# A decoder layer with a mixture of experts on one core: first products of the experts two ahead, double buffers, weights loaded in two parts

## What is computed

```
h = layernorm(x)                                   # 1024 x 256
scores = sigmoid(h @ gate_weight.T)                # 1024 x 16
weight_matrix = top 4 of 16 scores in the best 2 of 4 groups, normalised, x 2.5, else 0
g = einsum('th,nfh->ntf', h, gate_w);  u = einsum('th,nfh->ntf', h, up_w)   # 16 routed experts, f = 128
routed = einsum('ntf,nhf,tn->th', silu(g) * u, down_w, weight_matrix)
shared = silu(h @ sh_gate_w.T) * (h @ sh_up_w.T) @ sh_down_w.T              # f = 256: two more experts of 128
x = x + routed + shared
```

## Time and profile before

| what | value |
|---|---|
| median of 3 runs | 598.18 us (596.38 to 601.23) |
| the profiled execution | 597.41 us |
| its span on the core | 595.5 us |
| PE busy | 557.4 us (94%) |
| DVE busy | 437.1 us (73%) |
| ACT busy | 398.3 us (67%) |
| POOL busy | 298.9 us (50%) |
| share of PE in the chain that ended last | 83% |

### The profile page before, as it was taken

The page is one execution under the profiler, slowest core; times in us unless marked ns, Lnnn a source line. Parts: engine busy times, 40 slices in busy tenths (PEclk is TensorE's granted clock), DMA queues, the critical chain, the costliest instruction groups (busy, mean ns, idle before and its releaser), DMA issues.

```text
span 595.5 us, 10331 instructions
## 1 busy us (share of the span) xinstructions
PE 557.4 (94%) x3392; PEld 488.2 (82%) x3392; DVE 437.1 (73%) x1046; ACT 398.3 (67%) x783; POOL 298.9 (50%) x201
## 2 busy tenths in 40 slices
PE   3899999999999999999999999897777799999996
PEld 1687889989989989989989988786566688888885
DVE  8778989989989988998998998968593433333334
ACT  4978988878978979879779778665531433343331
POOL 2434756746746646656666563301041655556542
PEclk9998999999999999999999999999998899999999
DMA  6122032032032032032031020110002433333311
GB/s 206 29 107 81 0 117 81 1 116 81 2 117 81 2 116 81 2 116 75 8 116 56 27 97 23 59 29 1 0 1 70 149 105 107 104 123 113 108 62 70
DMA packets 16267, 42.23 MB, mean 71 GB/s; under 512 B 4544, under 2 KB 4800, under 8 KB 16224
## 3 DMA queue, kind: packets, MB, share of 16 engines
q1 hardware_dynamic: 16224, 41.69, 20.9%
HBM read 40.47 MB, written 1.21 MB: 70 GB/s over the span
## 4 chain that ended last, share of the span: by engine, by line
PE 83%; DVE 8%; ACT 4%; DMA 2%; issue 2%; SPq 1%; ACTq 0%; DVEq 0%
PE bank L1258 20%; PE bank L1260 19%; PE bank L1259 19%; PE bank L1254 15%; PE bank L1396 5%; PE bank L1384 4%; ACT tok L624 2%; DMA xbias<-in_xb 1%; DMA w_raw<-in_w 1%; DVE stats L976 1%; DVE xT_lo L911 1%; DVE gated_lo L1158 1%; ACT values L538 0%; DVE x L1248 0%; DVE raw L995 0%
## 5 line engine op out<-in xcount | busy, mean ns | idle before, releaser
L1258 PE MATMUL bank<-xT_lo,w_hi 128*128 128x512 f32 x336 | 140.0, 417 | 3.6 <-DVE conv L1149 1.3
L1260 PE MATMUL bank<-xT_hi,w_hi 128*128 128x512 f32 x336 | 132.3, 394 | 0.0
L1259 PE MATMUL bank<-xT_hi,w_lo 128*128 128x512 f32 x336 | 131.8, 392 | 0.0
L425 POOL TENSOR_TENSOR gated_lo<-gated,gated_hi 128x512 fp32r<-128x512 f32 x30 | 38.7, 1290 | 116.5 <-ACT gated_hi L644 112.8
L624 ACT ACTIVATE tok<-bank,nmr,rstd 128x128 f32<-128x128 f32 x256 | 91.0, 504 | 2.1 <-DVE nmr L891 2.1
L502 POOL TENSOR_TENSOR gate<-conv,tap 128x512 f32<-128x512 f32 x36 | 46.4, 1291 | 84.5 <-DVE conv L1149 71.4
L1258 PEld LDWEIGHTS bank<-xT_lo,w_hi 128*128 128x128 f32 x336 | 63.5, 189 | 18.8 <-DVE conv L995 3.2
L1260 PEld LDWEIGHTS bank<-xT_hi,w_hi 128*128 128x128 f32 x336 | 63.3, 188 | 14.2
L420 POOL TENSOR_TENSOR conv<-tap,conv 128x506 f32<-128x506 f32 x32 | 61.9, 1934 | 21.8 <-DVE conv L995 21.8
L420 POOL TENSOR_TENSOR raw<-tap,raw 128x506 f32<-128x506 f32 x32 | 61.9, 1934 | 20.3 <-DVE raw L995 16.3
L1259 PEld LDWEIGHTS bank<-xT_hi,w_lo 128*128 128x128 f32 x336 | 63.7, 190 | 9.6
(11 more groups left out here) (167 smaller groups left out, 1358.3 us busy)
## 6 DMA issues: line engine op xcount, KB each, us to landing
w_raw<-in_w SPq DMA_DIRECT2D x34, 384.0 KB, 4.4
obet<-obet_rows SPq DMA_DIRECT2D x16, 768.0 KB, 4.2
tap<-route_rows SPq DMA_DIRECT2D x16, 512.0 KB, 3.6
wv_raw<-in_wv SPq DMA_DIRECT2D x8, 256.0 KB, 4.8
wo_raw<-in_wo SPq DMA_DIRECT2D x8, 256.0 KB, 4.9
x<-in_x SPq DMA_DIRECT2D x2, 512.0 KB, 4.6
out_x<-x SPq DMA_DIRECT2D x4, 256.0 KB, 2.4
raw<-in_ctx SPq DMA_DIRECT2D x1, 512.0 KB, 5.4
```

The lines of the kernel that those rows point to most:

```text
L425: nc.gpsimd.tensor_tensor(gated_lo[:, cc], gated[:, c * N:(c + 1) * N], gated_hi[:, cc].bitcast(F32), ALU.subtract).then_inc(gated_lo_read ...
L1258: nc.tensor.matmul(o, l_hi, r_lo, start=start, stop=False, skip_group_check=loose)
L1259: nc.tensor.matmul(o, l_lo, r_hi, start=False, stop=False, skip_group_check=loose)
L1260: return nc.tensor.matmul(o, l_hi, r_hi, start=False, stop=stop, skip_group_check=loose)
```

## The change

It has five parts, all in the expert block.

1. PE makes the first products two experts ahead: the loop is `gate_up(n + 2)`, `down(n)` in place of `gate_up(n + 1)`, `down(n)`. Around the router, `gate_up(1)` is cut into its four banks, `gate_up(3)` stands in one piece before the weights' transposes, and `down(2)` is split around them.
2. `silu_g`, `prod`, `act_w`, `act_hi`, `act_lo` have two buffers, used in turn. `act_high(n)` and `down_high(n)` wait for `down(n - 2)`.
3. A weight load is two transfers: gate and up (256 KB, `load_gate_up`) once the low part of expert n - 2's gate and up is made, and down (128 KB, `load_down`) once `down_low(n - 2)` is.
4. The shared experts are not multiplied with ones: POOL's memset and four `weigh` are gone, and `act_high` reads `prod`.
5. Experts 3 and 4 are split early: ACT makes their high parts (128 x 768 each) behind `context_soft(1)`, POOL their low parts once the first half of `x_mixed` is there, into the free tiles `wv_hi/lo` and `wo_hi/lo`. The loads of experts 5 and 6 follow at once, their low parts on POOL wait for the end of the router (`r_ready`).

```diff
             sp.wait_ge(w_lo_ready, H + 2)
             load_expert(4, 1)
+            for n in (5, 6):
+                sp.wait_ge(w_lo_ready, n - 2 + H)
+                load_expert(n, 1 - n % 2)
...
+            def load_route(e, s):
+                if not (isinstance(e, int) and e < 2):
+                    sp.wait_ge(e_weighted, e * NCH - NCH)
...
+            def load_gate_up(n, s):
+                sp.wait_ge(w_lo_ready, n + (H - 2))
...
+            def load_down(n, s):
+                sp.wait_ge(down_lo_ready, n - 6)
...
+            load_route(0, 0)
+            load_route(1, 1)
+            load_gate_up(7, 0)
+            load_route(2, 0)
+            load_down(7, 0)
+            load_gate_up(8, 1)
+            load_route(3, 1)
+            load_down(8, 1)
+            with sp.Fori(0, E_ROUTED // 2 - 3) as r:
+                for s in range(2):
+                    load_gate_up(r * 2 + (9 + s), s)
+                    load_route(r * 2 + (4 + s), s)
+                    load_down(r * 2 + (9 + s), s)
             for s in range(2):
-                load_route(s, s, NCH * (s + 1))
-            with sp.Fori(0, E_ROUTED // 2 - 1) as r:
-                for s in range(2):
-                    expert_split(r * 2 + (3 + s))
-                    load_expert(r * 2 + (5 + s), s)
-                    load_route(r * 2 + (2 + s), s, r * (2 * NCH) + NCH * (3 + s))
+                load_route(E_ROUTED - 2 + s, s)
...
# POOL
-            pool.wait_ge(p_added, TT // 2)
-            nc.gpsimd.memset(wbc, 1.0).then_inc(ones_ready, 1)
...
+            pool.wait_ge(x_mixed, 1)
+            early_low(3)
+            early_low(4)
+            pool.wait_ge(r_ready, 1)
+            gate_up_low(5, 0)
+            gate_up_low(6, 1)
+            def step(n, m, s, up=True, down=True):
+                pool.wait_ge(ld_route[s], n * 8 - (1 + s) * 8)
+                weigh(n, m, s, 0)
+                if up:
+                    gate_up_low(n + 1, 1 - s)
+                weigh(n, m, s, 1)
+                if down:
+                    down_low(n, s)
...
# ACT
+            def step(n, m, s, up=True):
+                gate_silu(n, m)
+                if up:
+                    gate_up_high(n + 1, 1 - s)
+                act_high(n, m)
+                down_high(n, s)
...
# PE
+            down(1, 1, 0)
+            gate_up(3, 0)
+            down(2, 2, 1, (0,))
...
+            down(2, 2, 1, (1,))
             pe.wait_ge(r_tr_ready, NCH)
-            gate_up(3, 0, chunks=(1,))
             gate_up(4, 1)
-            down(3, 0, False, False)
-            with pe.Fori(0, E_ROUTED // 2 - 1) as r:
+            gate_up(5, 0)
+            down(3, 3, 0)
+            gate_up(6, 1)
+            down(4, 4, 1)
+            with pe.Fori(0, E_ROUTED // 2 - 2) as r:
                 for s in range(2):
-                    gate_up(r * 2 + (5 + s), s)
-                    down(r * 2 + (4 + s), 1 - s, False, False)
-            down(E_ALL, 1, False, True)
+                    gate_up(r * 2 + (7 + s), s)
+                    down(r * 2 + (5 + s), 5 + s, s)
+            down(E_ALL - 1, E_ALL - 1, 0)
+            down(E_ALL, E_ALL, 1)
```

More of the change, by code:

```diff
@@ L229, in decoder_layer @@
         ld_w = [sem(f"ld_w{i}") for i in range(2)]
+        ld_down = [sem(f"ld_down{i}") for i in range(2)]
         ld_prm = [sem(f"ld_prm{i}") for i in range(G)]
@@ L525, in _, with early_low, weigh @@
-            with pool.Fori(0, E_ROUTED // 2 - 1) as r:
+            def early_low(n):
+                hi, lo = early(n)
+                s = 1 - n % 2
+                pool.wait_ge(w_hi_ready, n + H)
+                nc.gpsimd.tensor_tensor(lo, w_raw[:, s * 3 * D:(s + 1) * 3 * D], hi.bitcast(F32),
+                                        ALU.subtract).then_inc(w_lo_ready, 1)
+            def weigh(n, m, s, c):
+                pool.wait_ge(u_prod, n * NCH + (c + 1 - NCH))
+                if not (isinstance(n, int) and n < 5):
+                    pool.wait_ge(e_hi, n * NCH + (c + 1 - 3 * NCH))
+                    pool.wait_ge(e_lo, n * NCH + (c + 1 - 3 * NCH))
+                nc.gpsimd.tensor_tensor(weighted(m, c), prod[:, two(m, c)],
+                                        wbc[:, s * T + c * N:s * T + (c + 1) * N],
+                                        ALU.mult).then_inc(e_weighted, 1)
@@ L802, in _, with router_scores @@
                 half_out(2, c, xT_hi)
-            for c in range(NCH):
+            def router_scores(c):
                 act.wait_ge(r_full, c + 1)
@@ new lines, in gate_up @@
+                if isinstance(n, int) and n in (3, 4):
+                    hi, lo = early(n)
+                for c, j in parts:
+                    if not (isinstance(n, int) and n == 1):
+                        pe.wait_ge(g_silu if j == 0 else u_prod, n * NCH + (c + 1 - 2 * NCH))
+                    for kt in range(KT):
+                        o = j * D + kt * P
+                        ins = mm3(e_ring[2 * c + j][:, :], hi[:, o:o + P], lo[:, o:o + P],
+                                  xs_(xT_hi, kt, c * N, (c + 1) * N), xs_(xT_lo, kt, c * N, (c + 1) * N),
+                                  kt == 0, kt == KT - 1)
+                    ins.then_inc(e_full, 1)
@@ new lines, in down @@
+            def down(n, m, s, chunks=range(NCH)):
+                hi, lo = w_hi[:, s * 3 * D:(s + 1) * 3 * D], w_lo[:, s * 3 * D:(s + 1) * 3 * D]
+                if m in (3, 4):
+                    hi, lo = early(m)
+                elif m > 4:
+                    pe.wait_ge(down_lo_ready, n - 4)
+                o = 2 * D
+                for c in chunks:
+                    pe.wait_ge(e_lo, n * NCH + (c + 1 - NCH))
+                    for t in range(G * c, G * (c + 1)):
+                        tt = slice(m % 2 * T + t * P, m % 2 * T + (t + 1) * P)
+                        ins = mm3(y_acc[t // 2][:, (t % 2) * D:(t % 2 + 1) * D], act_hi[:, tt], act_lo[:, tt],
+                                  hi[:, o:o + D], lo[:, o:o + D], m == 1 and t % 2 == 0, m == E_ALL, loose=True)
+                        if m == E_ALL and t % 2:
+                            ins.then_inc(y_full, 1)
+                    if m < E_ALL and c == NCH - 1:
+                        ins.then_inc(e_down, 1)
```

238 lines of the change are left out of this document (119 added, 119 removed).

## The result

| | median of runs, us | span, us | ratio to before, 95% interval |
|---|---|---|---|
| before | 598.18 (596.38 to 601.23) | 595.5 | |
| changed kernel | 626.97 (626.19 to 631.39) | 625.2 | 1.049 (1.039 to 1.060) |

The change costs 28.8 us. The forecast was 620 (606 to 634). In the changed kernel the waits over the whole span name the loop. The columns are engine, line, for whom it waited; total us, times, longest.

What follows compares the result with a forecast made beforehand. PE bounded the kernel before, at 8.30 us per expert; the change closes a loop through SP of 11.4 us. 466.8 + 12 x 11.4 = 603.6, plus 13.8 is a 617.4 span, forecast as 620 us (606 to 634).

Steps and rivals of the forecast that it cites:

- What bounds: Expert block: PE busy without a gap at 8.30 us per expert; about 16 us open around the router and at the end.
- Part 1, the router ends earlier: Router's chain on DVE: without POOL's work some 5.8 us go; weights' transposes at 448.0, 5.6 us earlier.
- the two low parts end before the small norm instructions begin: Early splits of experts 3 and 4 on POOL: claimed to cost nothing; without that cover, below 2 us.
- Part 2, the first experts: First routed experts: PE does not wait for weigh(3), and down_low(5) ends at 466.8 us.
- Part 3, the loop: Expert loop: each down_low waits for the one before through SP and a row transfer; 11.4 us a round against PE's 8.30.
- landing and start: Terms of the expert round: the row lands in 4.0 us, then POOL starts in 0.05.
- The hold-up: Term of the expert round: POOL and DVE delay each other at act_low, 0 to 0.6 us, taken as 0.3.
- Part 4, the end: After 12 rounds down_low(17) ends at 603.6; 13.8 us more give a span of 617.4.
- one spell a round at nothing: PE in the expert loop: a half-clock spell costs 1.5 us per round, but 9.8 stays under 11.4.
- The signs: Changed profile: transposes near 448, gate_up(7) near 475, steps 11 to 12 us, PE near 75% busy, weigh released by tap.
- The loop does not bind: Rival, expert loop: the row is in place when weigh wants it, PE never waits, 583 us; chance 0.06.
- The clock did not become the bound: Rival, expert loop: PE's clock falls to half throughout, 14.5 us per expert, 659 us; chance 0.04.

Runs made afterwards that it cites:

- POOL under the router: Row-early kernel plus eight idle 128x512 multiplications on POOL from the start of the router's chain on DVE: 592.4 us.
- row-early kernel: Changed kernel with only SP's order altered, each routing row issued right behind the same expert's down load: 584.06 us, 0.976 of before.
- the low part behind both halves: Changed kernel with gate_up_low(n + 1) on POOL moved behind both weigh instead of between them: 623.86 us, ratio 1.043.
- the row ahead of the gate/up load: Changed kernel with the routing row issued ahead of the gate/up load, still behind the down load of expert n + 2: 623.67 us, ratio 1.042.
- the smaller row: Changed kernel with each routing row broadcast to 16 partitions (64 KB) in place of 128 (512 KB): 606.67 us.
- the weights whole: Row-early kernel with routed weights from expert 7 on loaded whole (384 KB) behind down_low(n-2), not in two parts: 587.08 us, ratio 0.983.
- the early low parts later: Changed kernel with POOL's early low parts of experts 3 and 4 waiting for the third add of x_mixed: 629.3 us, ratio 1.051.

## Why the prediction was right, point by point

**What bounds.** Right: PE had no gap before, and everything turned on whether it got new ones.

**Part 1, the router ends earlier.** The chain on DVE, first and last instruction:

```profile
434.28 0.29 DVE L1250 TENSOR_TENSOR obet<-obet 128x128 f32<-128x128 f32 x1 [2.17 <-ACT obet L873]
...
447.38 0.29 DVE L1309 TENSOR_TENSOR obet<-obet 128x128 f32<-128x128 f32 x1
```

13.4 us in place of 19.2: the 5.8 us went as forecast, and the cause is shown by the kernel with POOL under the router. Score transposes were forecast at 430.7 and stood at 433.27, the weights' transposes at 450.62 (448.0). The distance between the two is 17.35 (17.3 forecast), so in this profile the miss of 2.6 us lies ahead. It is two spells of half clock (0.53 at 413 to 416 us, 0.50 at 423 to 426, both 1.00 before). Without them the row-early kernel, which has the same front, had its score transposes at 430.60 in its second profile. But that was no gain of 2.6: there the spell came behind the wait for the second sigmoid, the distance was 18.98, and the weights' transposes stood at 449.58. So the step that was mis-sized is the clock around the router: the sum had no spell there, and each of the two profiles has at least 1.6 us of them. The second sigmoid's wait, 1.92 us, was seen. That "the two low parts end before the small norm instructions begin" was wrong (409.11 to 412.69 against 410.98), but without a price where they stand.

**Part 2, the first experts.** PE did not wait until `gate_up(7)`, which began at 477.71 (near 475). `down_low(5)` ended at 469.97 (466.8): 2.6 from the front, 0.6 of its own. Its terms add up to 466.65; the 466.8 is a slip of 0.15.

**Part 3, the loop.** Right in mechanism, and settled by two runs: taking the wait from ahead of the row gives back all of it (43 us), and a smaller row shortens each round by what it lands earlier. The terms, in the round shown above: SP 0.17 (0.18), issues 1.16 (1.05), landing and start 3.99 (4.05), `weigh`, `gate_up_low`, `weigh` with the hold-up 4.21 (4.09), ACT 1.05 (1.04), `down_low` 0.94 (1.02): 11.52. The mean of 12 was 11.61, forecast 11.4: 2.5 us in all. The hold-up that I put at 0.3 is 0.45, the second `weigh` at 1.74 in place of 1.29. In the means of the 12 rounds, landing and start are 4.03 (4.05) and all behind them 6.17 (6.15); what is left of the miss is SP and its issues, 1.41 (1.23), mostly 1.33 and 1.7 in turn.

**Part 4, the end.** From `down_low(17)` to the end of the span 15.9 us, forecast 13.8. `gate_up(18)` took 7.2 us (605.73 to 612.91) for its 5.5: a spell of half clock after a wait of 3.11. I had put one spell a round at nothing, since PE waits there anyway. That holds inside the rounds, where one came only in about every second, but the last spell has no wait behind it to hide in. That there was one is chance: in three of the other four profiles with this loop (the low part behind both halves, the row ahead of the gate/up load, the smaller row) the last `gate_up` took 5.6 us.

Together 3.2 + 2.5 + 2.1 = 7.8 us on a forecast span of 617.4: the 625.2 measured. In the time, 620 against 626.97. More than half of this (2.6 and 1.6) is half clock at places where PE's delay is not hidden. All misses went the same way, and the width of the range took them in; the loop itself was sized to 0.2 us a round.

**The signs.** `weigh` was released by the transfer of `tap`, 5.4 us behind the end of `down_low` in the mean (5.2 forecast), the steps were 11.2 to 12.2 us, and SP's long wait was that of the down load (115.8 us in 12 waits). PE was busy 80.88% and not 75%, because matmuls at half clock count as busy; it did 416 of 581 matmuls, 72%. One of the signs of being wrong came as well: the router ended after 450, at 450.62, by the spells of part 1. And one landing of the 13 from 470 us on took over 5 us (5.5; the median is 3.7).

**The rivals.** "The loop does not bind" at 583 us is close to what the row-early kernel does (584.06), so the sum for it was about right, and its chance low for the right reason. The clock did not become the bound (0.93 in the loop, against the 0.73 from which it would), but it took its part. The figures of the Trainium skill made the round 0.4 shorter; the median landing of 3.8 lay between their 3.6 and my 4.0.

## What to carry to other kernels

On an in-order queue that waits, ask of each transfer which step's end it stands behind, and follow the wait round: if what the transfer feeds leads back to that same step one iteration later, its latency is paid in each iteration, however far ahead the compute engines work. Take a landing from a stage with the same traffic, not from a busier one. Before taking a term out of a loop, work out the next loop under it: the term is worth no more than the difference between the two. And price a wait on PE with the half clock behind it: here the wait for the second sigmoid was 1.92 us, and taking it out gave 2.7.

## What the runs showed of the hardware

The clock after a pause differs between executions of one kernel. The row-early kernel, first and second profile, over the same stretch:

```profile
413.00:416.00 3.00, 3.00 (x9) 2.39 (x10) 2.24 (x12) 1.09 (x2) 0.00 (x0) 0.56 0.47 155
```
```profile
413.00:416.00 3.00, 3.00 (x16) 2.64 (x15) 2.66 (x12) 1.09 (x2) 0.00 (x0) 1.00 0.45 133
```

PE's pauses ahead of it are the same in both (1.71 and 0.74 us), yet the clock is 0.56 in one and 1.00 in the other. The score transposes stood 2.55 us apart, the weights' transposes and the ends of the spans only 0.9, and the medians of the two groups 0.1. The kernels with the change showed the spell in six profiles and not in five. Those six had the full clock behind the wait for the second sigmoid (1.00 from 431 to 438 us); three of the other five, the row-early kernel's second, the weights whole and the smaller row, had the spell there (0.76). So a spell that is absent at one wait came at the next. What decides where it falls is open. "TensorE: Matmul & The Clock Gate" of the Trainium skill (Part 1) says that the number of slow matmuls at a kernel's start differs from run to run; the trace agrees, and shows the same in the middle of a kernel. A difference of 2 us in one profile's front is thus no evidence for an edit.

Transfers issued close together on one queue delay each other. 256 KB issued ahead of the row landed in 2.7 us, and in 4.4 when issued 0.5 us behind its 512 KB. For the row itself the difference is less clear: 3.8 us with the 256 KB ahead and 4.3 with them behind, but also 4.2 with them ahead in the profile with the early low parts later.
